# Second convolution: pairs of mirrored products stacked on 64 partitions by on-chip transfers, 64-row matmul tiles over two images, and two images stored early

## What is computed

```python
def _L1_conv_ref(x, filters):            # filters (32, 32, 10, 10)
    spot = _extract_patches(x, 3, 1, 1)  # 3x3 window around each pixel
    spot = concatenate([ones, spot], -1) # 10 values
    feat = spot[..., :, None] * spot[..., None, :]      # 100 products
    return einsum('bcyxf,ocf->boyx', feat, filters)
x = x + _L0_conv_ref(_gn(x), w3, b3, w5, b5, wr, br)    # 3x3 and 5x5 convolution, mixed
x = x + _L1_conv_ref(_gn(x), filters)
```

## Time and profile before

| | |
|---|---|
| median of 3 runs | 301.25 us (300.67 to 302.45) |
| the profiled execution's own time | 300.6 us |
| its span in the trace | 298.9 us |
| PE busy | 273.2 us, 91% of the span |
| DVE busy | 252.5 us, 84% |
| ACT, POOL busy | 87.5 us, 29.8 us |
| DMA | 11.45 MB in all, mean 38 GB/s |
| granted TensorE clock, mean | 0.985 |

### The profile page before, as it was taken

One profiled execution on the slowest core, in us unless ns is written; L12 is line 12 of the kernel. 1 busy time (PEld: TensorE's weight loads), 2 busy tenths in 40 slices (PEclk: granted clock), 3 DMA queues, 4 the chain that ended last, 5 costly groups with the idle time before them and its releaser, 6 DMA issues.

```text
span 298.9 us, 13564 instructions
## 1 busy us (share of the span) xinstructions
PE 273.2 (91%) x6464; PEld 131.0 (44%) x6464; DVE 252.5 (84%) x220; ACT 87.5 (29%) x135; POOL 29.8 (10%) x78
## 2 busy tenths in 40 slices
PE   0499999999989999999999999999999999999930
PEld 0234343444435444363556575353445446477310
DVE  3899899998999889799999999975999999970330
ACT  4532016989079889348000000004000000000000
POOL 5804970000110000000000000000000000000000
PEclk9999999999999999999999999999999999999995
DMA  6974000000000000000000000084000000000049
GB/s 172 383 202 104 5 2 2 2 5 2 4 2 2 4 4 2 2 2 5 2 4 2 4 2 4 2 182 105 2 2 4 2 2 4 2 4 4 2 92 189
DMA packets 19206, 11.45 MB, mean 38 GB/s; under 512 B 17744, under 2 KB 17872, under 8 KB 19024
## 3 DMA queue, kind: packets, MB, share of 16 engines
q1 hardware_dynamic: 14640, 9.06, 12.0%
q10 hardware_dynamic: 4512, 1.53, 2.2%
HBM read 6.40 MB, written 4.19 MB: 35 GB/s over the span
## 4 chain that ended last, share of the span: by engine, by line
PE 71%; DVE 16%; ACT 3%; issue 3%; DMA 3%; SPq 1%; DVEq 0%; ACTq 0%
PE acc L1028 63%; PE acc L1071 5%; DVE product L657 3%; ACT raw L511 3%; DMA raw<-in_x 3%; PE acc L1141 2%; DVE stats L761 2%; DVE scaled L657 1%; DVE plane L779 1%; DVE raw L821 1%; PE acc L1122 1%; DVE product L892 1%; DVE product L683 1%; DVE product L689 1%; DVE arena L689 1%
## 5 line engine op out<-in xcount | busy, mean ns | idle before, releaser
L1028 PE MATMUL acc<-product,weight 32*32 32x512 f32 (+1 forms) x3072 | 126.9, 605 | 0.3 <-DVE product L892 0.3
L1028 PEld LDWEIGHTS acc<-product,weight 32*32 32x32 f32 (+1 forms) x3072 | 65.5, 110 | 59.1 <-issue 41.4
L899 DVE TENSOR_TENSOR product<-plane 128x4096 f32<-128x4096 f32 x19 | 83.2, 4420 | 0.1
L1028 PE MATMUL acc<-raw,weight 32*32 32x512 f32 (+1 forms) x960 | 45.3, 604 | 0.0
L1071 PE MATMUL acc<-product,middle 32*64 32x512 f32 (+1 forms) x576 | 29.9, 597 | 0.0
L1028 PEld LDWEIGHTS acc<-raw,weight 32*32 32x32 f32 (+1 forms) x960 | 20.7, 112 | 20.2 <-issue 15.7
L821 DVE TENSOR_TENSOR raw<-acc,arena 128x512 f32<-128x512 f32 x16 | 9.9, 684 | 16.7 <-issue 16.5
L1028 PE MATMUL acc<-product,arena 32*32 32x512 f32 (+1 forms) x448 | 22.2, 604 | 0.0
L899 DVE TENSOR_TENSOR raw<-plane 128x4096 f32<-128x4096 f32 x5 | 22.1, 4416 | 0.0
L511 ACT ACTIVATE raw<-arena 32x512 f32<-32x512 f32 x32 | 21.8, 680 | 0.5
L541 ACT ACTIVATE arena<-acc 128x2048 f32<-128x2048 f32 x2 | 3.8, 1878 | 61.2 <-PE acc L1028 61.2
(11 more groups left out here) (122 smaller groups left out, 212.2 us busy)
## 6 DMA issues: line engine op xcount, KB each, us to landing
raw<-in_x SPq DMA_DIRECT2D x8, 512.0 KB, 8.8
out<-raw SPq DMA_DIRECT2D x24, 128.0 KB, 3.0
arena<-in_L_conv_filters SPq DMA_DIRECT2D x4, 400.0 KB, 7.6
out<-raw ACTq DMA_DIRECT2D x8, 128.0 KB, 4.7
arena<-in_L_conv_w ACTq DMA_DIRECT2D x4, 100.0 KB, 4.3
w_in<-in_L_conv_w ACTq DMA_DIRECT2D x2, 36.0 KB, 1.9
w_in<-in_L_conv_w SPq DMA_DIRECT2D x2, 36.0 KB, 2.2
b_in<-in_L_conv_b SPq DMA_DIRECT2D x2, 0.5 KB
```

Source lines behind the costliest of these rows:

```text
L899: nc.vector.tensor_tensor(both_halves(g, u), plane_halves(g), plane_halves(g, PRODUCTS[k][0] * PITCH + PRODUCTS[k][1]), ALU.mult)\
L1028: return nc.tensor.matmul(acc[32 * s:32 * (s + strips), j, r, :], weights[32 * r:32 * r + 32, t:t + strips, :] .rearrange("p t c -> p (t c ...
```

## The change

1. The order of `PRODUCTS` changes, so that the four products (1,1), (2,1), (1,2), (2,2) ("twins") and their mirror images (1,-1), (2,-1), (1,-2), (2,-2) have their taps next to one another in `weight1`.
2. The mirror product is made one or two pixels shifted (`multiply_twins`): its taps then lie on the same pixels as those of its twin. DVE makes as many product images as before, of the same size.
3. SP moves blocks of 32 partitions (`swap`): six transfers of 32 x 4358 elements (558 KB) for each twin. Afterwards one home holds, on partitions 0 to 63 and 64 to 127, the twin's and the mirror's channels of images 0 and 2; another those of images 1 and 3.
4. PE takes the twins with tiles of 64 rows (`twin_column`): 4 matmuls of 64 by 64 in a round of pairs, 8 of 64 by 32 in a round of singles. A round covers two images and two products where it covered four images and one product, so the number of rounds is the same: 36 in each group.
5. `mirror_taps` on ACT copies the mirror's taps to partitions 32 to 63 and 96 to 127 of `weight1`; POOL writes two more sets of stream borders (`plane[0]`, `raw[0]`).
6. Units and homes are ordered anew; `plane[0]` is a seventh home in group 1.
7. The last unit ends by images: 1 and 3 are evicted and stored while PE is still at 0 and 2.

```diff
+            def swap(g, u):
+                first, mirror, swapped = home(g, u), home(g, u + MIRROR), home(g, u + SWAPPED)
+                sp.wait_ge(stream_made, made(g, u))
+                wait_emptied(sp, g, u + SWAPPED)
+                for p in (0, 64):
+                    sp.dma_start(swapped[p:p + 32, 0:2 * HALF_LEN], first[p + 32:p + 64, 0:2 * HALF_LEN])\
+                      .then_inc(crossed[g][u], 16)
+                sp.wait_ge(stream_made, made(g, u + MIRROR))
+                for p in (32, 96):
+                    sp.dma_start(swapped[p:p + 32, 0:2 * HALF_LEN], mirror[p:p + 32, 0:2 * HALF_LEN])\
+                      .then_inc(swapped_filled[g][u], 16)
+                sp.wait_ge(crossed[g][u], 32)
+                for p in (0, 64):
+                    sp.dma_start(first[p + 32:p + 64, 0:2 * HALF_LEN], mirror[p:p + 32, 0:2 * HALF_LEN])\
+                      .then_inc(filled[g][u], 16)
+            for u in TWIN_ORDER[0]:
+                swap(0, u)
             for r in range(GROUP):
                 sp.wait_ge(evicted, GROUP + r + 1)
                 store(sp, 0, r, range(STRIPS))
+            for u in TWIN_ORDER[1]:
+                swap(1, u)
...
+MOVED = ({ONE_TWO: TWO_ONE, TWO_TWO: ONE_ONE, TWO_TWO + SWAPPED: ONE_TWO},
+         {TWO_TWO: TWO_ONE, ONE_ONE + MIRROR: ONE_TWO})
+TWIN_ORDER = ((TWO_ONE, ONE_ONE, ONE_TWO, TWO_TWO), (TWO_ONE, ONE_TWO, TWO_TWO, ONE_ONE))
...
+            def multiply_twins(g, u):
+                down, right = PRODUCTS[u - 5]
+                multiply(g, u)
+                wait_free(g, u + MIRROR)
+                nc.vector.tensor_tensor(both_halves(g, u + MIRROR), plane_halves(g, right),
+                                        plane_halves(g, down * PITCH), ALU.mult).then_inc(stream_made, 1)
...
+                if (g, u) == (1, LINEAR):
+                    wait_moved(dve, 0, TWO_TWO)
+                if (g, u) == (1, NEXT):
+                    dve.wait_ge(half_done, 2)
...
+                def tile(h, s, strips, d, t, last_one):
+                    return nc.tensor.matmul(acc[32 * s:32 * (s + strips), j, 2 * h + odd_images, :],
+                                            weights[64 * h:64 * h + 64, t:t + strips, :]
+                                            .rearrange("p t c -> p (t c)"), pixels(h, SIDE_ROWS * (s // 2) + d),
+                                            start=False, stop=last_one, tile_position=(64 * h, 32 * s))
...
+            def wait_twins(g, u, odd_images):
+                pe.wait_ge(mirrored, 2)
+                if odd_images:
+                    pe.wait_ge(crossed[g][u], 32)
+                    pe.wait_ge(swapped_filled[g][u], 32)
+                else:
+                    pe.wait_ge(filled[g][u], 32)
...
+                if g == 0:
+                    whole_unit(g, BELOW, (SINGLES, PAIRS)).then_inc(unit_used, 1)
+                    whole_unit(g, FAR_BELOW, (SINGLES,)).then_inc(unit_used, 1)
+                    for u in TWIN_ORDER[0]:
+                        twin_unit(g, u, 1, (SINGLES, PAIRS)).then_inc(unit_used, 1)
+                        twin_unit(g, u, 0, (PAIRS, SINGLES)).then_inc(unit_used, 1)
+                    wait_made(g, FAR)
...
```

More of the change, by code:

```diff
@@ L84 @@
[L84 to L91 removed]
+              BELOW: 3, FAR_BELOW: 0, FAR: 2,
@@ L228, in conv_kernel @@
         unit_used = sem("unit_used")
+        mirrored = sem("mirrored")
+        crossed = [{u: sem(f"crossed{g}_{u}") for u in TWINS} for g in range(NG)]
+        filled = [{u: sem(f"filled{g}_{u}") for u in TWINS} for g in range(NG)]
+        swapped_filled = [{u: sem(f"swapped_filled{g}_{u}") for u in TWINS} for g in range(NG)]
         stored = sem("stored")
@@ L342, in _ @@
                 store(sp, 0, r, range(STRIPS))
-            for r in range(GROUP):
-                sp.wait_ge(evicted, 3 * GROUP + r + 1)
+            for u in TWIN_ORDER[1]:
+                swap(1, u)
+            for r, count in LAST_EVICTED:
+                sp.wait_ge(evicted, count)
                 store(sp, 1, r, (0, 1))
@@ L470, in _ @@
             stream_borders(raw[1]).then_inc(borders, 1)
+            pool.wait_ge(stream_made, made(0, FAR))
+            pool.wait_ge(square_ready, 1)
+            pool.wait_ge(shared_done, 1)
+            stream_borders(plane[0]).then_inc(borders, 1)
+            pool.wait_ge(stored, 16 * GROUP * STRIPS)
+            stream_borders(raw[0]).then_inc(borders, 1)
         @block.scalar
@@ L589, in _ @@
             keep_whole(1)
+            mirror_taps()
             spread(0, 1, range(GROUP - 1))
@@ L608, in _ @@
             keep_cross(1)
-            for r in range(GROUP):
-                act.wait_ge(evicted, 3 * GROUP + r + 1)
+            for r, count in LAST_EVICTED:
+                act.wait_ge(evicted, count)
                 store(act, 1, r, (2, 3))
@@ new lines, in twin_taps @@
+            def twin_taps(g, j, u, odd_images, pairs, stop=False):
+                k = u - 5
+                ys, where = rows_of(PRODUCTS[k]), columns_of(PRODUCTS[k])
+                tile = home(g, u + SWAPPED) if odd_images else home(g, u)
+                for n, ix in enumerate(where):
+                    at = FIRST1[k] + n * len(ys)
+                    half, shift = (j + ix) % 2, (j + ix) // 2
+                    last = twin_column(j, odd_images, twin_pixels(tile, half, shift), ys,
+                                       weight1[:, at:at + len(ys), :], stop and n == len(where) - 1, pairs)
+                return last
@@ L1218, in _, with twin_unit @@
+            def twin_unit(g, u, odd_images, forms, stop=False):
+                wait_twins(g, u, odd_images)
+                if len(rows_of(PRODUCTS[u - 5])) == 1:
+                    forms = (SINGLES,)
+                for pairs in forms:
+                    twin_taps(g, 0, u, odd_images, pairs, stop and pairs == forms[-1])
+                    last = twin_taps(g, 1, u, odd_images, pairs, stop and pairs == forms[-1])
+                return last
             for g in range(NG):
@@ L1284, in _ @@
                     side_unit(g, 1, "next", SINGLES).then_inc(unit_used, 1)
-                    in_pairs = False
-                for u in range(7, LAST_UNIT):
-                    wait_made(g, u)
-                    if len(rows_of(PRODUCTS[u - 5])) == 1:
-                        forms = (False,)
-                    else:
-                        forms = (in_pairs, not in_pairs)
-                    for pairs in forms:
-                        taps1(g, 0, u, pairs)
-                        last = taps1(g, 1, u, pairs)
-                    last.then_inc(unit_used, 1)
-                    in_pairs = forms[-1]
```

209 lines of the change are left out of this document (140 added, 69 removed).

## The result

The changed kernel takes **342.3 us** (median of 4 runs, 341.5 to 343.5) against 301.85 for the kernel before on the same chip (4 runs, 300.7 to 304.0): a ratio of 1.134, with 1.126 to 1.141 as the 95% interval. The forecast was 343, in its own range of 331 to 364. The profiled execution took 343.5 us, its span is 341.8.

A forecast was written before the change was run, and what follows sets the result against it. PE bounded the kernel; its 14.6 us gain would be outweighed by transfers of 15.7 us a twin. PE's end 329.0 plus tail 7.6 gave 336.6, with clock 4 a span of 340.6, so 343 us; range 303 to 385, the forecast's own 331 to 364.

The forecast's parts named there:

- the rate: SP's transfers within SBUF: 213 GB/s taken, 2.62 us a transfer, 15.7 us a twin; main forecast's chance 0.60.
- the full overlap: Rival on SP's transfers: partitions 0 and 64 overlap at 412 GB/s, 8.1 us a twin, 293 us in all; chance 0.16.
- what the Trainium skill says of two transfers: SP's transfers: concurrent ones at partitions 0 and 64 gain only 6%, about 226 GB/s, 14.8 us a twin, total 9 lower.
- The landings: Twins' transfers: PE waits for every landing, longest group 0 gaps 8 and 10 us; last swapped home lands at 314.6.
- PE's arrival at the twins: Group 0: after side terms, (1,0) and (2,0), PE reaches the twins at about 149, with no wait yet.
- Group 0 to group 1: DVE's first group 1 operation waits for the last transfer (204.0); halves and eviction follow, PE starts accumulating at 213.2.
- PE's gain: Twins' 48 rounds in singles need 16 records in place of 32: 48 x 0.20 = 9.6 us less of PE.
- The tail: After PE's end: early stores take 1.05 MB off it, 5.0 us less, leaving 12.5 - 5 = 7.6 us.
- The clock: PE at half pace after long gaps: 2 us each for (2,2) with (0,2) and the last twin, 4 in all.
- Reads and writes that share their way: Rival on SP's transfers: below 180 GB/s; 396 us at 150, 469 at 107; chance 0.14.
- 64-row tiles are slow: Rival on PE's twin rounds: 64-row tiles slower or no faster than 32-row ones, about 2 us at the end; no chance given.
- the signs named at the end: Changed profile: DMA share 1 at 200 to 215 GB/s, PE's DMA gaps some 60 us, PE busy 80%, clock below 1.

The follow-up runs named there:

- the wide kernel: The changed kernel with each pair of 32 x 4358 transfers replaced by two in-place blocks of 128 partitions by 1089 elements, crossing left out: 294.9 us, ratio 0.977.
- two queues: The changed kernel with transfers to partitions 64 to 127 issued by ACT on its own queue beside SP's: 338.7 us, ratio 1.122.
- the kernel with 64 elements: The changed kernel with each transfer moving only 64 elements of each row, waits and matmuls the same: 289.9 us, ratio 0.959.
- the two-product version with ACT's copies: The changed kernel with only (2,1), (1,1) and their mirrors stacked, and ACT copying the crossed blocks, 16 transfers left: 303.8 us, ratio 1.007.
- the best version: Two stacked products with ACT's copies, plus plain products before stacked ones in group 0 and (1,1)'s group 1 transfers cut in four: 295.3 us, ratio 0.980.
- the kernel with quarter rows: The changed kernel with each 32-partition transfer cut along the row into four of 1089 or 1090 elements: 350.2 us, ratio 1.158.
- the one with all crossings by ACT: The changed kernel with ACT copying the crossed blocks of all eight stacked products, SP's transfers down from six to four per twin: 317.4 us, ratio 1.054.

## Why the prediction was right

**What bounds it, and the rate.** 213 GB/s from the filter loads and the last stores, against 207 to 223 measured. The step that this rests on, taking the block of 32 partitions as the near case and not the 412 GB/s of 128 partitions, is what the wide kernel shows (372 in place of 223, 47 us). The last stores, which mix both halves on two queues, were the right argument against the full overlap: two queues brought 3.6 us, within intervals that overlap. By what the Trainium skill says of two transfers (6% more; the section that the prediction names) the total would have come out lower by 9 us as the prediction has it, by 7 as its own eight twins of 0.9 us give (by the same sum 230 GB/s is 334 us and not 331); the measured total was not lower with one queue, though the rate of 223 in group 1 lies on its side.

**The landings.** By my working (2,1) would land at 149.5, (1,1) at 165.2, (2,2) at 198.7 and 203.9, the last twin at 314.6. PE's rows after these waits start at 151.96, 167.38, 200.15 and 205.21, 316.64: 1.3 to 2.5 us later, with the same pattern. The first landings took longer than a flow of 2.62 us and 1.5 of latency, and the flow in group 0 was slower between 160 and 186 us than in group 1 (207 and 223). (1,2), forecast for 181.0, was not waited for, since PE was still busy until 183.8; the prediction had PE wait for every landing. PE's arrival at the twins, forecast at 149, was 149.2.

**Group 0 to group 1.** DVE waited for the last transfer until 205.19 (204.0 forecast), and PE started group 1 at 215.04 (213.2). The wait of 14.0 us on DVE, with three halves and the eviction behind it, is the step that carries group 0's loss into group 1, as the text had it.

**PE's gain.** 9.6 us were forecast for the 48 rounds. In the kernel with 64 elements the two stretches named above take 61.8 and 90.6 us, 4.6 and 3.6 less than before: **8.2 us**, though a wait of 0.5 us stands in them. The mechanism (64-row singles at the pace of pairs) is right, and the size 1 us too high. The tail is 4.8 us shorter in that kernel (7.8 against 12.6), 5.0 forecast.

**The clock.** 4 us were forecast, 2 in each group. In the group 0 part it cost at most 0.4 on the path: PE's matmuls after the gaps are at half pace (windows 167 to 172 and 200 to 209 have a granted clock of 0.52 and 0.50, the 1.2 GHz level), but DVE reached its eviction only 0.41 us before PE was ready for it (212.30, above), so DVE's lateness covers the rest. At the end it cost 2.6: 96 matmuls took 10.03 us from 316.64 on, where the same group took 7.42 in the kernel with 64 elements. So this term was too high by 1.0 to 1.4, and the last landing came 2.0 us later than forecast; the two nearly cancel, and PE's end came at 334.0 where the text had 329.0 and 4 for the clock. That the total came within 1 us is luck to that extent; the mechanism and the rate are not. The tail of 7.8 us was forecast at 7.6.

**What was missing.** The code loads (5.7 us of gaps in group 1) and SP's longer issues appear in no term. They cost nothing here that the trace shows, since both lie in stretches where the landings set the end and the DMA engines stay full (213 to 220 GB/s from 286 to 315). In the two-product version with ACT's copies the gap of 3.53 us, PE's waits for transfers (0.90, 2.01 and 1.09 us) and the slower matmuls after one of them (1.6 us) add up to 9.1 us, about what my figure was low by (8 to 12).

**The rivals.** Full overlap is the wide kernel: 293 forecast, 294.9 measured, at the rate from which the text let it decide. Reads and writes that share their way fall with the same run: 372 GB/s from SBUF to SBUF. That 64-row tiles are slow falls with the weight loads. Of the signs named at the end, one was off: PE's waits for DMA sum to 34.7 us, not some 60. Four gaps are of 5.9 to 8.6 us where the text had six of 7 to 10; the rest of the loss stands as DVE's waits and as matmuls at the lower clock.

## What to carry to other kernels

Price a transfer within SBUF by the partitions it spans, not by its bytes alone: the same bytes ran at 372 GB/s over 128 partitions and at 222 over 32 or 64, and neither a second queue nor shorter rows changed that. Before trading instructions of a saturated engine for transfers, compare the transfers' time for one piece of work with the time of the engine that supplies that piece (here 15 us against 8.8), and look whether a subset can hide: two products of four nearly did (waits of 1.3 and 1.0 us are left). And when an edit bundles two things, price them apart: of the 6 us that the best version gains, 5 stand in the tail that the early stores shorten.

## What the runs showed of the hardware beyond that

- **Code loads and long rows.** In the second convolution TensorE stood still for 0.4 to 5.2 us in the middle of units with all data present where rows of 8.7 or 17 KB kept the DMA engines full, and not where rows of 4.4 KB moved at up to 373 GB/s. The packets of 16 KB of the "instruction" queue use the same engines, and each of the 17 gaps ended 2.4 to 2.9 us after one.
- **An issue can block its engine.** SP's issues of transfers (one line of the program; duration ns min/median/max) grow when others are queued; in the chain the steps from 297.4 to 304 us are such issues:

```profile
L400 SPq DMA_DIRECT2D raw<-raw x4: 507/1624/2334, 163.4 to 267.6; - x4
L400 SPq DMA_DIRECT2D product<-raw x2: 586/606/625, 137.5 to 138.2; - x2
```

- **A short wait can be paid twice, and need not be.** After a wait of 2.0 us the next 64 matmuls took 5.40 us in place of 3.79 (window 155 to 165 of that version with a granted clock of 0.83), and after 2.8 us in the changed kernel 5.05. But after waits of 2.5 and 3.0 us in the kernel with quarter rows, and of 2.6 us in the one with all crossings by ACT, they took 3.79, and in the wide kernel 96 matmuls after 2.9 us took 7.42, at full clock. What decides it is not shown; a forecast that adds up waits alone can be too low by 1.6 us for a wait of 2.0.
- **ACT's copy** of 32 partitions by 4358 elements took 3.85 us, longer than a transfer of the same block in full flow (558 KB at 222 GB/s, 2.5 us).
